# Order of the attention body: projections gathered behind the turned probabilities, the second value projection made one body sooner

## The reference

```python
shift, scale, gate = parts of silu(c) @ W_mod + b_mod         # per sequence
h = layernorm(x) * (1 + scale) + shift
q, k, v = split(h @ W_qkv, 3)                                 # 16 heads of 64
attn = softmax(q @ k.T * 64 ** -0.5)                          # per head, 128 x 128
x = x + gate * ((attn @ v) @ W_out + b_out)
```

## Time and profile before

| | |
|---|---|
| median of 3 runs | 643.22 us (642.95 to 643.85) |
| the profiled execution | 643.25 us, span 641.7 us |
| PE busy | 622.9 us, 97% of the span |
| DVE busy | 506.9 us, 79% |
| ACT busy | 479.6 us, 75% |
| POOL busy | 290.7 us, 45% |
| granted TensorE clock | full in every slice |
| first scores (S2) of body 0, and of the last body | at 24.33 us, and at 402.62 us |

### The profile page before, as it was taken

One profiled execution on the slowest core, in us unless ns is written; L12 is line 12 of the kernel. 1 busy time (PEld: TensorE's weight loads), 2 busy tenths in 40 slices (PEclk: granted clock), 3 DMA queues, 4 the chain that ended last, 5 costly groups with the idle time before them and its releaser, 6 DMA issues.

```text
span 641.7 us, 17325 instructions
## 1 busy us (share of the span) xinstructions
PE 622.9 (97%) x5580; PEld 539.4 (84%) x5580; DVE 506.9 (79%) x1116; ACT 479.6 (75%) x1722; POOL 290.7 (45%) x354
## 2 busy tenths in 40 slices
PE   7899999999999999999999999889998999999997
PEld 7778888888898888888888888779987888888886
DVE  4887887878788878778787887878866888888886
ACT  5887877877978878778779797758876656565653
POOL 4353444443443534444534434536654355445552
PEclk9999999999999999999999999999999999999999
DMA  7212011010110110110101102023342121222111
GB/s 237 66 31 52 12 48 42 19 44 17 44 44 8 44 49 12 44 39 21 44 13 48 44 1 63 15 62 98 111 137 66 50 65 40 64 65 65 33 34 34
DMA packets 54531, 32.50 MB, mean 51 GB/s; under 512 B 15185, under 2 KB 52321, under 8 KB 54497
## 3 DMA queue, kind: packets, MB, share of 16 engines
q1 hardware_dynamic: 52864, 27.85, 16.0%
q0 software_dynamic: 1632, 4.21, 2.1%
HBM read 25.74 MB, written 6.31 MB: 50 GB/s over the span
## 4 chain that ended last, share of the span: by engine, by line
PE 89%; DVE 5%; SPq 2%; ACT 2%; issue 1%; DMA 0%; ACTq 0%; DVEq 0%
PE banks L601 10%; PE banks L627 9%; PE banks L612 8%; PE banks L1893 7%; PE banks L572 6%; PE banks L576 4%; PE banks L573 4%; PE banks L1306 4%; PE banks L1865 3%; PE banks L585 3%; PE banks L1879 3%; PE banks L1853 2%; PE banks L648 2%; PE banks L587 2%; PE banks L586 2%; PE banks L649 2%
## 5 line engine op out<-in xcount | busy, mean ns | idle before, releaser
L518 POOL TENSOR_TENSOR late_blocks<-late_blocks,p_rsum 128x512 f32<-128x512 f32 x128 | 130.5, 1040 | 209.8 <-DVE p_rsum L934 209.8
L813 ACT ACTIVATE late_blocks<-banks,neg_max 128x128 f32<-128x128 f32 x512 | 182.4, 392 | 2.9 <-DVE neg_max L927 2.9
L813 ACT ACTIVATION_READ_ACCUMULATOR late_blocks<-banks,neg_max 128x1 f32 x512 | 119.5, 233 | 0.0
L791 ACT ACTIVATE wide<-banks 128x512 f32<-128x512 f32 x127 | 78.2, 617 | 39.2 <-PE banks L576 34.2
L947 DVE CAST oT_hi<-banks 128x512 fp32r<-128x512 f32 x60 | 41.5, 692 | 64.4 <-PE banks L627 64.4
L572 PE MATMUL banks<-xT_hi,w_qkv_hi 128*128 128x256 f32 x256 | 82.4, 322 | 1.7 <-DVE xT_lo L922 0.8
L927 DVE TENSOR_REDUCE neg_max<-banks 128x8 f32<-128x1024 f32 x64 | 77.2, 1206 | 1.2
L601 PE MATMUL banks<-wide 64*128 64x128 f32 x1024 | 74.4, 285 | 0.0
L576 PE MATMUL banks<-xT_hi,w_qkv_lo 128*128 128x256 f32 x256 | 71.7, 280 | 0.1
L573 PE MATMUL banks<-xT_lo,w_qkv_hi 128*128 128x256 f32 x256 | 71.5, 279 | 0.0
L601 PEld LDWEIGHTS banks<-wide 64*128 64x128 f32 x1024 | 62.1, 187 | 10.7 <-issue 7.8
(11 more groups left out here) (172 smaller groups left out, 1556.5 us busy)
## 6 DMA issues: line engine op xcount, KB each, us to landing
early<-in_mask SPq DMA_DIRECT2D x16, 220.0 KB
early<-in_mask SPq DMA_DIRECT2D x80, 44.0 KB
x_in<-in_x SPq DMA_DIRECT2D x16, 128.0 KB, 2.2
x_res<-in_x SPq DMA_DIRECT2D x16, 128.0 KB, 2.2
x_scratch<-x SPq DMA_DIRECT2D x16, 128.0 KB, 1.9
f_x_in<-x_scratch SPq DMA_DIRECT2D x16, 128.0 KB, 2.4
f_x_res<-x_scratch POOLq DMA_DIRECT2D x16, 128.0 KB, 2.8
x_scratch<-f_x POOLq DMA_DIRECT2D x16, 128.0 KB, 2.2
```

The lines of the kernel that those rows point to most:

```text
L518: pool.tensor_tensor(p[:, par, heads, :], p[:, par, heads, :], p_rsum[:, par, heads].unsqueeze(2).broadcast_to([128, 4, T]), ALU.mult).the ...
L791: act.activation(dst, proj_ps[k % 2], ACT.Copy).then_inc(proj_saved[k % 2], 1)
L813: act.activation(p[:, par, m, :], s_ps[par][:, e, j, :], ACT.Exp, bias=neg_max[:, par, 4 * e + j:4 * e + j + 1], accum_out=p_sum[:, par, m ...
```

## The change

On PE, a body's projections are put together so that they always follow a `turn_p`: T1, then Q4 to Q7; T2, then Q8, Q9, V10; T3, then Q11, Q12, V13, V14, V15. Before, Q4, Q8 and Q11 stood apart from their neighbours, and V15 stood behind S2 of the next body. `turn_p` does group 1 before group 0. One task more, V15 of pair 0, is made ahead of body 0, and one fewer in the last body. On ACT the saves Q4 to Q7 stand together ahead of the exponentials of unit 3; of the exponentials of unit 5 two are left in the body and six stand at the next body's start, behind the save of V15, which now waits until P3 has read its part of `v`; two of unit 4 come later. The first exponential of a unit now waits for the second transposed group that reads the same buffer. On DVE, `save_turned` 0 is put ahead of `invert_sums` 1, `row_max` 4 behind `save_turned` 2, the label sums behind `save_oT` 2, and `invert_sums` 4 behind the normalised x. In the last body `row_max` 2 is put ahead of `invert_sums` 1.

The diff, cut to its core:

```diff
-    V1, XT, OUT, QK0, QK1, V0 = ((14, 1), 2, 3, (4, 5, 6, 7), (8, 9, 11, 12), (10, 13))
-    TASKS = 14
+    V1, XT, OUT, QK0, QK1, V0 = ((14, 15), 2, 3, (4, 5, 6, 7), (8, 9, 11, 12), (10, 13))
+    TASKS = 15
...
             scores(i, 2, i - 1, QK1)
-            project_v(i, V1[1], 1, 1)
+            turn_p(i, 0, 1)
             turn_p(i, 0, 0)
-            turn_p(i, 0, 1)
...
             scores(i, 3, i - 1, QK1)
+            turn_p(i, 1, 1)
+            turn_p(i, 1, 0)
             if nxt:
                 pe.wait_ge(xT_split, i * 2 + 4)
-                project_qk(i, QK0[0])
-            turn_p(i, 1, 0)
-            turn_p(i, 1, 1)
-            if nxt:
-                for k in QK0[1:]:
+                for k in QK0:
                     project_qk(i, k)
             probs_v(i, 1)
 
             if nxt:
+                scores(i, 4, i, QK0)
+            turn_p(i, 2, 1)
+            turn_p(i, 2, 0)
+            if nxt:
                 project_qk(i, QK1[0])
-                scores(i, 4, i, QK0)
-            turn_p(i, 2, 0)
-            turn_p(i, 2, 1)
-            if nxt:
                 project_qk(i, QK1[1])
                 project_v(i, V0[0], 0, 0)
             probs_v(i, 2)
 
             if nxt:
                 scores(i, 5, i, QK0)
+            turn_p(i, 3, 1)
+            turn_p(i, 3, 0)
+            if nxt:
                 project_qk(i, QK1[2])
-            turn_p(i, 3, 0)
-            turn_p(i, 3, 1)
-            if nxt:
                 project_qk(i, QK1[3])
                 project_v(i, V0[1], 0, 1)
                 project_v(i, V1[0], 1, 0)
+                project_v(i, V1[1], 1, 1)
             probs_v(i, 3)
...
         project_v(-1, V1[0], 1, 0)
+        project_v(-1, V1[1], 1, 1)
...
+        def save_second_v(i):
+
+            zero_wait(act, turn_full[0], i * 8 + 8)
+            save_v(i, V1[1], 1, 1)
...
                 act.wait_ge(max_ready, i * 4 + (unit + 1))
+                if unit >= 2 and not (isinstance(i, int) and i == LAST):
+                    act.wait_ge(turn_full[0], i * 8 + (2 * unit - 3))
...
-            save_v(i, V1[1], 1, 1)
+            save_second_v(i - 1)
+            exps(i, 1, 2, 6)
             save_turned(i, 0)
             exps(i, 2, 0, 8)
...
-            if nxt:
-                save_qk(i, QK0[0])
             save_turned(i, 1)
             if nxt:
-                save_qk(i, QK0[1])
-            exps(i, 3, 0, 2)
-            if nxt:
-                save_qk(i, QK0[2])
-            exps(i, 3, 2, 2)
-            if nxt:
-                save_qk(i, QK0[3])
-            exps(i, 3, 4, 4)
+                for k in QK0:
+                    save_qk(i, k)
+            exps(i, 3, 0, 8)
...
-                exps(i, 4, 4, 4)
-
-                save_qk(i, QK1[2])
+                exps(i, 4, 4, 2)
             save_turned(i, 3)
             if nxt:
+                save_qk(i, QK1[2])
                 save_qk(i, QK1[3])
-                exps(i, 5, 0, 4)
                 save_v(i, V0[1], 0, 1)
-                exps(i, 5, 4, 4)
+                exps(i, 4, 6, 2)
                 save_v(i, V1[0], 1, 0)
+                exps(i, 5, 0, 2)
...
             row_max(i, 2)
+            save_turned(i, 0)
             invert_sums(i, 1)
-            save_turned(i, 0)
             if nxt:
                 modulate(i)
...
             save_turned(i, 3)
             if second_next:
                 ln_apply(i + 2)
+            if nxt:
+                invert_sums(i, 4)
             save_oT(i, 3)
...
         def last_body():
 
+            row_max(LAST, 2)
             invert_sums(LAST, 1)
             ffn.parts["moments_first"](dve)
-            row_max(LAST, 2)
```

More of the change, by code:

```diff
@@ L421, in attention_phase @@
     turn_saved = [sem(f"turn_saved{n}") for n in range(2)]
-    V1, XT, OUT, QK0, QK1, V0 = ((14, 1), 2, 3, (4, 5, 6, 7), (8, 9, 11, 12), (10, 13))
-    TASKS = 14
+    V1, XT, OUT, QK0, QK1, V0 = ((14, 15), 2, 3, (4, 5, 6, 7), (8, 9, 11, 12), (10, 13))
+    TASKS = 15
     def in_body(i, k):
+        if k < XT:
+            return False
         if i < 0:
-            return k not in (V1[1], OUT)
+            return k != OUT
         if i == PAIRS:
             return k == OUT
-        return k == V1[1] or (i > 0 if k == OUT else i < PAIRS - 1)
+        return i > 0 if k == OUT else i < PAIRS - 1
     def task_count(i, k):
@@ L618, in probs_v @@
             if half:
-                wait_saved(pe, i - 1 + b, V1[b])
+                wait_saved(pe, i - 1, V1[b])
             else:
@@ L725, in last_probs_v @@
             if half:
-                wait_saved(pe, LAST - 1 + b, V1[b])
+                wait_saved(pe, LAST - 1, V1[b])
             else:
@@ L741, in last_body @@
             scores(LAST, 2, LAST - 1, QK1)
-            project_v(LAST, V1[1], 1, 1)
             turn_last(0, 0)
@@ L847, in body @@
                 save_v(i, V0[0], 0, 0)
-                exps(i, 4, 4, 4)
-                save_qk(i, QK1[2])
+                exps(i, 4, 4, 2)
             save_turned(i, 3)
             if nxt:
+                save_qk(i, QK1[2])
                 save_qk(i, QK1[3])
-                exps(i, 5, 0, 4)
                 save_v(i, V0[1], 0, 1)
-                exps(i, 5, 4, 4)
+                exps(i, 4, 6, 2)
                 save_v(i, V1[0], 1, 0)
+                exps(i, 5, 0, 2)
         def last_body():
-            save_v(LAST, V1[1], 1, 1)
+            save_second_v(LAST - 1)
+            exps(LAST, 1, 2, 6)
             act.wait_ge(turn_full[1], LAST * 4 + 1)
@@ L884, in scalar @@
         save_qk(-1, QK1[3])
-        exps(0, 1, 0, 8)
+        exps(0, 1, 0, 2)
         save_v(-1, V1[0], 1, 0)
@@ L1003, in body @@
             invert_sums(i, 3)
-            if nxt:
-                row_max(i, 4)
             if second_next:
@@ L1011, in body @@
                 ln_aggregate()
+            if nxt:
+                row_max(i, 4)
+            save_oT(i, 2)
             edges.parts["sum_labels"](dve, i)
-            save_oT(i, 2)
             if nxt:
                 row_max(i, 5)
-                invert_sums(i, 4)
             save_turned(i, 3)
```

## The result

The changed kernel takes 654.24 us (median of 4 runs, 653.64 to 654.45), the kernel before beside it 643.09 us (4 runs, 642.72 to 643.85). The ratio is 1.0168, with a 95% interval of 1.0156 to 1.0181: 1.7% slower. The forecast was 651.0 in a range of 646.5 to 656. So sign and range held, and the forecast was 3.2 us short of an increase of 11.15.

The account below looks back on a forecast made before the run. PE was taken to bound the kernel. Per body -0.54 + 0.70 - 0.26 + 0.48 + 0.05 = +0.43, so +6.0 for 14 bodies; with +1.8 and +0.3 at the ends, 8.1 on 643.25: about 651 us, range 646.5 to 656.

Parts of the forecast that it names:

- Start of the body: S2 to B: 6.43 instead of 6.97 us, 0.54 shorter, with PE waiting 0.20 at B for `gatedT`.
- The copy loses to POOL: Rival, chance 0.08: POOL gets in ahead of `shift_scale`; a body costs 1.3 us more, 663.8 in all.
- B is in time: Rival, chance 0.12: B comes when PE is there; a body is +0.23 us, 647 to 648.5 in all.
- V15 uncovered: V15, moved to the run behind T3, costs its 0.70 us a body there, with nothing covering it.
- changes of tile: Q4, Q11 and Q8 in the rest of the body save 0.04, 0.04 and 0.18: together -0.26 us a body.
- hand-overs: Half-bank waits in projection runs: new ones at V10, V13 and V15, V14's gone, together +0.48 us a body.
- the rival that saves standing together would be free: Rival, chance 0.08: banks come back without a wait once ACT's saves stand together; -0.54 us a body, 638 in all.
- The rule that counts changes of mode alone: Counting only tiling-mode changes on PE, 14 before and 13 after, the whole change saves one, about 0.18 us a body.
- Unit 4's last exponentials at 0: Unit 4's exponentials behind V13's save cost 0: a wait up to 0.1 us at T0 is swallowed at B.
- The second half of the transposes: Group 0 of T0, T2 and T3 needs DVE's copies: 0 to 0.06 us each, 0.05 taken for all.
- Start of the program: V15 ahead of body 0 puts S2 1.2 us later; body 0 keeps 0.9, its later part adds 0.92: +1.8.
- The last body: In the last body unit 1's sums are inverted later, mostly covered by the maximum put ahead: +0.3 us (0 to 0.4).

Follow-up runs that it names:

- e3: The changed kernel with the small copy `gate_cols` put ahead of the reciprocal that releases POOL; 653.17 us in one execution.
- e4: The changed kernel with `invert_sums` 1 put ahead of `save_turned` 0 again, as before the change; 663.91 us in one execution.
- e2: The changed kernel with the saves of Q4, Q5, Q8, Q11, Q12 and V13 cut to 256 of 512 columns in looped bodies; 643.65 us in one execution.
- e7: The changed kernel with transposes' group 0 inside the projection runs and unit 4's last exponentials ahead of V13's save; 642.20 us, ratio 0.9986.
- e5: The changed kernel with V15 put back behind S2 of the next body, projections still gathered; 655.48 us, ratio 1.0191.
- e1: The changed kernel without DVE's second copy of the output of units 1 and 2 in looped bodies; 650.54 us in one execution.
- e6: The kernel before with V15 alone moved behind V14, its save at the next body's start, nothing gathered; 670.14 us, ratio 1.0425.
- e9: The changed kernel with transposes' group 0 inside the projection runs, V15 back behind S2, and ACT's saves and exponentials reordered; 633.58 us, ratio 0.9849.

## Why the prediction was right, and where it was short

**Start of the body: right, term and mechanism.** Forecast 6.43 from S2 to B, measured 6.43. `shift_scale` 0.12 and `gate_cols` 0.38 are as forecast (0.16 and 0.35 or more); e3 and e4 move the copies across POOL's start and the time follows. "The copy loses to POOL" is what e4 measures. DVE's part was forecast to a few hundredths, so this is no luck. "B is in time" did not come by itself; e3 makes it come, and it gives 0.08 a body and not the 0.20 of the forecast, since T0's wait for POOL (0.12, below) then stands in PE's way: 6.23 + 0.12 = 6.35.

**V15 uncovered, changes of tile, hand-overs: right in sum and in each stretch.** S3 to S4: Q8's 0.71 leaves, with 0.22 of changes of tile; 7.16 - 0.93 = 6.23, measured 6.22. S4 to S5: 4.55 + 0.71 (Q8) + 0.24 (V10's hand-over) = 5.50, and with T2's 0.12 5.62, measured 5.63. S5 to S2: 6.26 + 0.70 (V15) + 0.24 (the fifth hand-over) - 0.04 = 7.16, and with T3's 0.12 7.28, measured 7.28. That V10, V13 and V15 do wait refutes the rival that saves standing together would be free, and e2 shows what they wait for. The rule that counts changes of mode alone (one fewer, 0.18) falls short of the 0.26: S3 to S4 alone shows 0.23 of it (7.16 - 0.71 - 6.22), and that stretch differs by no more than 0.03 from body to body.

**Unit 4's last exponentials at 0: right here, by little.** T0 starts 207.32 - 206.10 = 1.22 behind S2 where a T behind S otherwise starts at 1.10: a wait of 0.12, a little above the 0.1 that the forecast allowed. It is POOL's: its work on unit 4 ends at 207.19, and in e7, where it ends 1.07 ahead of T0, T0 starts 1.09 behind S2. It is swallowed at B, where PE waits 0.08 instead of 0.20. e5 shows what it costs once V15 stands there again and nothing is waited for behind it.

**The second half of the transposes: the step that was mis-sized.** "Cost 0 to 0.06 each; I take 0.05 for all." Measured are 0.12 at T2, 0.12 at T3, and nothing that counts at T0: 0.24 to 0.26 a body (after, e1). Against the 0.05 taken that is 0.19 x 14 = 2.7 us more, while all bodies together came out 8.4 - 6.0 = 2.4 above the forecast; the stretches' roundings make the rest. The bound was too tight. It compared DVE's end with PE's way and let group 0 start when the copy ends. In the trace the copy ends at 220.66, and group 0, last in a T that began at 220.22 and whose last four starts stand 0.11 apart, begins at about 220.80. PE had come to it at about 220.71, just behind the copy's end, so by the forecast's reckoning there was nothing to wait for. But it took 0.14 from DVE's end to the first transpose, against the 0.05 or 0.06 with which PE followed ACT's saves and DVE's `gatedT` (212.48 to 212.54). In e6 T0 follows the same copy by 0.15 (214.10 to 214.25). Why PE follows this copy later than the other results is open.

**Start of the program: short by 0.46.** S2 of body 0 came 1.33 later, not 1.2, which is within what this start differs by from one execution to the next. Body 0 gave nothing of it back: it took 25.08 instead of 24.15, +0.93, which is just the 0.92 of its later part. The assumption that its own waits would absorb 0.3 was wrong. The last body cost 0.24 for the 0.3 forecast. By the terms 2.4 (bodies) + 0.46 - 0.06 = 2.8, and 651.3 + 2.8 = 654.1, the profiled execution (654.15). The rest of the 3.2 is the rounding of 651.3 to 651.0.

What stays open is V14's slow first step in e9, the 0.14 behind DVE's copy, and why body 0 absorbed nothing of its late start; none was tried by itself.

## What to carry to other kernels

Before moving a filler, ask what it covered. V15 stood between two waits of other engines (POOL's at T0, DVE's at B); moved, it cost its full length (0.70) and a hand-over (0.25), and gained 0.53. Gathering like work saves changes of tile (0.04 to 0.18 each here), but with two half banks each third task in a row pays the difference between save plus signals and one task (0.24 here). Count both, and put other work of the same tile shape between: here that turned +0.60 a body into -0.21 (e7), and with V15 back at its old place and ACT's order mended into -0.69 (e9). A good place for a small copy is directly behind or ahead of the instruction that releases a long POOL job (0.12 to 0.16 here), and a bad one is behind the job's start (0.63 to 0.67).

## What the runs showed of the hardware that was not expected

- In the looped bodies a copy of 128 x 4 words on DVE takes 0.12 to 0.16 while POOL is idle, and lasts to the end of POOL's running instruction where there is one (0.38, 0.63, 0.67 by when it starts). Directly behind the reciprocal it starts 0.16 to 0.17 ahead of POOL and is not held.
- After each wait for a half bank PE's next step is 0.10 longer: 0.22 for 0.12, and 0.34 for 0.235. So a wait costs more than its gap. With half the save (e2) the first step still shows 0.26.
- A projection directly behind transposes starts only 0.03 behind the last of them, and its first step is then 0.08 longer: no net cost. In other places (behind P or S) the change of tile shows as a start 0.20 behind.
- A wait inside a group of like matmuls appears in no row of waits. Only the group's duration shows it (1.22 against 1.09 for eight transposes).
